# The end of the expert layers: gathers, a combine and key products put in another order

## The chip, the core and the metric

One core of a Trainium2 chip runs the whole program. The metric is the time of one execution on the device in microseconds; less is better. The chip's engines each run their own list of instructions in order and wait for one another through semaphores: TensorE (PE) does matrix products, VectorE (DVE) and ScalarE (ACT) do elementwise work, GpSimd (POOL) small work and the gathers of rows, and the queue of SyncE (SP) starts the transfers from memory.

## The reference

The input x is 625 rows of 512 numbers, with 10,000 edges. Four layers follow, each added to x:

```python
x = x + L0_gnn(layernorm(x), edges)      # two hyperbolic graph convolutions
x = x + L0_ffn(layernorm(x))             # eight experts, two for each row
x = x + L1_gnn(layernorm(x), edges)      # two plain graph convolutions
x = x + L1_ffn(layernorm(x))             # attention over 100 slots and two dense layers
```

The change lies at the end of the second layer and the start of the third. The expert layer is

```python
probs = softmax(xf @ gate_w.T + gate_b); topw, topi = top_k(probs, 2)
sel_w, sel_idx = top_k(wm.T, cap)              # each expert takes its 93 best rows
h = gelu(xg @ w1[e] + b1[e]); out = (h @ w2[e] + b2[e]) * sel_w
of = zeros(T, D).at[sel_idx].add(out)          # rows scattered back
```

with hidden size 2048. A graph convolution of the third layer gathers the normed rows over the edges with degree weights (here a product with a 625 x 628 matrix of edge counts) and multiplies by a 512 x 512 weight. The fourth layer needs, among much else, Wk times a 1024 x 100 matrix, the "keys"; they don't depend on x and are computed early.

## The kernel before, in words

Rows of x are five tiles of 125 (X[:, t, :]). Products in float32 are made of float32r halves: a high half is a copy (ACT), the low half the difference (DVE or POOL), and three products high*high, low*high, high*low are summed in one PSUM bank.

**Experts (`pe_moe`, `a_moe`, `v_moe`, `sp_moe`, `g_moe`).** For expert e there are eight 1 MB weight chunks, four of the first layer (`up(e, c)`, products 8e to 8e+3) and four of the second (`down(e, c)`). `sp_moe` loads chunk m + 8 into the slot of chunk m when `w_used` of m is there; behind the 64th come the two chunks of Wk (`N_TK`), the two weights of the third layer (`N_GNN1`) and four chunks of Wkv. The first six chunks of each expert are split into HW (ACT, high) and LW (DVE, low) by `weights(i)`; the last two are used as they are (down(e, 2) and down(e, 3)). PE's order for an expert is up 0, up 1, gelu 0 (four transposes of HS; ACT's Gelu reads them), up 2, gelu 1, up 3, gelu 2, down 0, gelu 3, down 1, dispatch of the next expert, down 2, gathered_T of the next, down 3. In `scale(e)` DVE adds the bias (OT), ACT multiplies by the gate weight (OS or OW), and for experts six and seven DVE makes the low half (OSL).

**Back to rows.** Experts 0 to 5 (`NB = 6`) write their scaled rows into a DRAM tensor `y_rows`, and since each row has at most two experts, POOL gathers them with two lists of indices: YL (five gathers of 125 rows, the lower expert) and YH (the higher one). DVE adds them to X in `back_low` and `back_high`. Experts 6 and 7 go back through a product with the transposed selection matrix PT, `combine(e)`: two matmuls for each row tile t into bank 3 + t, and DVE adds the bank to X. In before POOL starts YL when the outputs of expert five are written and the ranks of expert seven are known, YH when the gather product of expert seven is done. YL lies where the rank work's tiles were, YH where XFH was. Each engine's list for the last expert is:

- PE: up 0, combine(6), up 1, gelu 0, up 2, gelu 1, up 3, gelu 2, down 0, gelu 3, down 1, down 2, down 3; then keys 0 and 1, combine(7), keys 2 and 3, then `pe_first_aggregate`.
- DVE: combine(6)'s adds, `back_low`, the weights and gelu halves, `degrees`, `back_high`, `v_counts`, scale(7).
- ACT: weights, HS, Gelu, then `a_counts`, scale(7).

**Third layer's start.** CT holds the edge counts; `a_counts` makes GCH and `v_counts` GCL over the expert weights' places HW0 to HW3, and so waits for `w_used`. `v_gnn1` adds combine(7) to X with row sums (`total`), ACT makes squares, POOL the power, DVE the normed rows GU, ACT the high half GTH, DVE the low half GTL. The keys' high and low half A2H and A2L read PSUM bank 0, which is also bank 0 of the aggregate; so the aggregate's work on bank 0 waits for `key_v`. `pe_first_aggregate` goes by row tiles j over the eight banks with GCH, then GCL, and then GTL.

A wait on a semaphore counter is written `q.wait_ge(*count.of(key))`; `landed(n)` is the arrival of load n. PSUM banks are handed on by the dictionary `free`.

Of the kernel before, what the change touches and what calls it, by code (L numbers as in the profile page):

```python
# [130 lines left out]
def program(nc, I, out):  # L131
    T5, P, D, NP = 5, 125, 512, 628
# [8 lines left out]
    with ctx:  # L141
# [9 lines left out]
        place = {}  # L151
# [10 lines left out]
        def after(name):  # L162
            return place[name]
# [77 lines left out]
        def landed(n):  # L241
            return s_raw[slot_of(n)], raw_at[n]
# [825 lines left out]

        def split(m):
            return m % 8 < 6

# [3 lines left out]
        def chunk(i):  # L1077
            return 8 * (i // 6) + i % 6
# [45 lines left out]
        def g_moe(q):  # L1124
            q.wait_ge(*x1_done.of(4))
            g_layernorm(q, ln1, ln_stat, ln_pow, 1)
            q.iota(EO[:, :, :], [[CS, 6], [0, T5]])
            q.fill(LT8[:, :], 1.0)
            q.fill(BIGM[:, :], 1.0)
            q.iota(io94[:, :], [[1, CS]]).then_inc(*mconst.up("one"))  # L1130
            q.wait_ge(*mconst.of("one"))
            q.select(LT8[:, :].rearrange("p (a b) -> p a b", a=8), ALU.is_gt, 0.0, [[1, 8], [-1, 8]], 0)
            q.select(BIGM[:, :], ALU.is_gt, 0.0, [[-1, P]], 1)
            q.fill(io94[:, CAP:CS], -1.0).then_inc(*mconst.up("all"))
            q.wait_ge(*gate_pe.of("lg"))
            q.fill(ZR[:, :], 0.0).then_inc(*mconst.up("zero"))
            q.wait_ge(*code_v.of("low"))
            q.wait_ge(s_wrow, 32)
            q.wait_ge(s_yw[0], 32 * 3)
            q.wait_ge(s_yw[1], 32 * 3)  # L1140
            q.wait_ge(*rank_v.of(NE - 1, "po"))
            for t in range(T5):
                q.gather(YL[:, t, :], yrow, IL[:, t:t + 1]).then_inc(s_rows, 16)
            q.wait_ge(*ga_mm.of(NE - 1))
            for t in range(T5):
                q.gather(YH[:, t, :], yrow, IH[:, t:t + 1]).then_inc(s_back, 16)
# [3 lines left out]
        def a_moe(q):  # L1150
# [95 lines left out]
            for e in range(NE):  # L1246
                n = 6 * e
                up(e, 0)
                weights(n + 4)
                up(e, 1)  # L1250
                gelu(e, 0)
                weights(n + 5)
                up(e, 2)
                gelu(e, 1)
                weights(n + 6)
                up(e, 3)
                gelu(e, 2)
                weights(n + 7)
                gelu(e, 3)
                weights(n + 8)  # L1260
                if e + 1 < NE:
                    dispatch(e + 1)
                    gathered_T(e + 1)
                weights(n + 9)
                if e == NE - 1:
                    a_counts(q)
                scale(e)

        def v_moe(q):
# [209 lines left out]
                q.ts(ln2["rd"], ln2["rd"], 1.0 / D, None, ALU.mult).then_inc(*ln_stat.up(2, "rd"))  # L1479

            def combine(e):
                for t in range(T5):
                    q.wait_ge(*co_mm.of(e, t))
                    q.tt(X[:, t, :], X[:, t, :], PS[0:P, 3 + t, :], ALU.add).then_inc(*x2_done.up(e, t))

# [14 lines left out]
            rank_end(1)  # L1500
            for e in range(NE):
                n = 6 * e
                if e == NE - 1:
                    combine(NE - 2)
                    back_low()
                weights(n + 4)
                gelu(e, 0)
                weights(n + 5)
                if e == NB - 1:
                    places()  # L1510
                if e + 2 < NE:
                    rank_tiles(e + 2, (0, 1))
                gelu(e, 1)
                weights(n + 6)
                if e + 2 < NE:
                    rank_tiles(e + 2, (2, 3))
                weights(n + 7)
                if e + 2 < NE:
                    rank_tiles(e + 2, (4,))
                    rank_end(e + 2)  # L1520
                weights(n + 8)
                if e + 1 < NE:
                    dispatch(e + 1)
                    gathered_T(e + 1)
                weights(n + 9)
                if e == NE - 1:
                    degrees()
                    back_high()
                    v_counts(q)
                scale(e)  # L1530

        def pe_moe(q):
# [123 lines left out]
            def combine(e):  # L1656
                k = e % 2
                q.wait_ge(*os_hi.of(e))
                q.wait_ge(*pt_done.of(e))
                q.wait_ge(*os_lo.of(e))  # L1660
                for t in range(T5):
                    b = 3 + t
                    q.wait_ge(*free[b])
                    q.mm(PS[0:P, b, :], PT[:, k, P * t:P * t + P], OS[:, k, :], True, False)
                    q.mm(PS[0:P, b, :], PT[:, k, P * t:P * t + P], OSL[:, k, :], False, True).then_inc(*co_mm.up(e, t))
                    free[b] = x2_done.of(e, t)
# [7 lines left out]
            gathered_T(0)  # L1674
            for e in range(NE):
                up(e, 0)
                if e == NE - 1:
                    combine(NE - 2)
                up(e, 1)
                gelu(e, 0)  # L1680
                up(e, 2)
                gelu(e, 1)
                up(e, 3)
                gelu(e, 2)
                down(e, 0)
                gelu(e, 3)
                down(e, 1)
                if e + 1 < NE:
                    dispatch(e + 1)
                down(e, 2)  # L1690
                if e + 1 < NE:
                    gathered_T(e + 1)
                down(e, 3)
            pe_keys(q, (0, 1))
            combine(NE - 1)
            pe_keys(q, (2, 3))

# [6 lines left out]
        cols[0] = 0  # L1706
        GCH = at("gCH", [P, T5, NP], f32r, SCR)
        GCL = at("gCL", [P, T5, NP], f32r, after("gCH"))
        GUH = at("gUH", [128, 4, NP], f32r, after("gCL"))
        GUL = at("gUL", [128, 4, NP], f32r, after("gUH"))  # L1710
        GU = at("gU", [P, T5, D], f32, after("gUL"))
# [41 lines left out]
                g_power(q, ln2["rs"][:, t:t + 1], ln2["rs"][:, t:t + 1], hm[0:P, 0:1], ln_pow, 2, t)  # L1753

        def a_counts(q):
            q.wait_ge(*w_used.of(chunk(6 * NE - 1)))
            for m in range(T5):
                q.act(GCH[:, m, :], CT[:, m, :], ACT.Copy).then_inc(*gch_done.up(m))

        def v_counts(q):  # L1760
            q.wait_ge(*w_used.of(chunk(6 * NE - 1)))
            for m in range(T5):
                q.wait_ge(*gch_done.of(m))
                q.tt(GCL[:, m, :], CT[:, m, :], GCH[:, m, :].bitcast(f32), ALU.subtract).then_inc(*gcl_done.up(m))

        def a_gnn1(q):
# [7 lines left out]

            for t in range(3):
                squares(t)
            q.wait_ge(*key_mm.of("a2"))
            q.act(A2H[:, :, :], PS[:, 0, 0:4 * L].rearrange("p (a b) -> p a b", a=4), ACT.Copy).then_inc(*key_a.up("a2"))
            high(0)
            squares(3)  # L1780
            high(1)
            squares(4)
            for t in range(2, T5):
                high(t)
            for k in range(2):
# [17 lines left out]
        def v_gnn1(q):  # L1803
# [28 lines left out]
            total(3)  # L1832
            spread(2)
            normed(1)
            q.wait_ge(*key_a.of("a2"))
            q.tt(A2L[:, :, :], PS[:, 0, 0:4 * L].rearrange("p (a b) -> p a b", a=4), A2H[:, :, :].bitcast(f32), ALU.subtract).then_inc(*key_v.up())
            total(4)
            spread(3)
            normed(2)
            first_low(0)  # L1840
            spread(4)
            normed(3)
            first_low(1)
            normed(4)
            for t in range(2, T5):
                first_low(t)
            for k in range(2):
# [59 lines left out]
        def pe_first_aggregate(q):  # L1907
            def share(b, j, l, r, start, stop):
                f, h = b // 2, b % 2
                return q.mm(PS[:, b, 0:HALF], l[:, j, 128 * f:128 * f + 128], r[:, j, HALF * h:HALF * h + HALF], start, stop)  # L1910

            q.wait_ge(*gcl_done.of(4))
            for j in range(T5):
                q.wait_ge(*th_done.of("g", 0, j))
                for group in (((1, 2, 3, 4, 5, 6), (0, 7)) if j == 0 else (range(8),)):
                    for b in group:
                        if j == 0 and b >= 3:
                            q.wait_ge(*x2_done.of(NE - 1, b - 3))
                        if j == 0 and b == 0:
                            q.wait_ge(*key_v.of())  # L1920
                        share(b, j, GTH, GCH, j == 0, False)
                    for b in group:
                        share(b, j, GTH, GCL, False, False)
            for b in range(8):
                for j in range(T5):
                    q.wait_ge(*tl_done.of("g", 0, j))
                    i = share(b, j, GTL, GCH, False, j == 4)
                if b % 2:
                    i.then_inc(*gu_mm.up(0, b // 2))
# [1022 lines left out]
```

## Time and profile before

| | us |
|---|---|
| median of 3 runs | 2144.78 |
| lowest, highest | 2138.63, 2148.16 |
| the profiled execution | 2148.19 |
| its span, first to last instruction | 2146.4 |
| TensorE busy | 2089.4 (97%) |
| VectorE busy | 1491.4 (69%) |
| ScalarE busy | 1124.4 (52%) |
| GpSimd busy | 872.2 (41%) |

The expert layer takes the stretch from about 180 to 440 us of the span; the last expert from 407 to 440. All times in rows below are microseconds from the span's start, and durations of one instruction or of a merged row of several ("x5"). In square brackets stands how long the engine was idle before, and what released it.

### The profile page before, as it was taken

To read this page: it belongs to the slowest core of one execution; us is meant where nothing else is said; L and a number is where in the kernel's file an instruction comes from. 1 tells how busy PE (TensorE), PEld (TensorE's weight loads), DVE (VectorE), ACT (ScalarE), POOL (GpSimd) and SP (SyncE) were. 2 spreads that over 40 slices of the span, in tenths; PEclk is the share of its full clock that TensorE was granted. 3 is DMA by queue.
4 is the path that set the end of the run, shared out by engine and by line. 5 is a ranking of instruction groups with operands and counts; after the bars stand their busy time and mean duration, and the time that the engine had idled before them with its cause. 6 is when DMAs were issued, how large, how long until landed. Compare 5 with 4: busy or idle time off the path is not lost.

```text
span 2146.4 us, 35992 instructions
## 1 busy us (share of the span) xinstructions
PE 2089.4 (97%) x13282; PEld 1953.0 (91%) x13282; DVE 1491.4 (69%) x3179; ACT 1124.4 (52%) x3010; POOL 872.2 (41%) x704
## 2 busy tenths in 40 slices
PE   8887999998999999999999999999999999999998
PEld 7776666687799999999999999999999999999997
DVE  8656988754366677677666777767667677776676
ACT  4543676534454555555545555555455555554464
POOL 0000000201264555555544555555545555555461
PEclk9887999999999999999999999999999999999999
DMA  6000999940121111132111111222111112221110
GB/s 216 1 29 11 318 324 328 296 166 1 67 87 64 63 63 64 64 103 86 64 64 64 64 64 63 91 96 66 63 63 64 64 63 78 100 75 63 60 45 25
DMA packets 89162, 201.16 MB, mean 94 GB/s; under 512 B 8196, under 2 KB 12580, under 8 KB 88985
## 3 DMA queue, kind: packets, MB, share of 16 engines
q1 hardware_dynamic: 86746, 196.28, 26.9%
q0 software_dynamic: 2240, 2.57, 0.5%
q8 instruction: 106, 1.74, 0.4%
q14 instruction: 70, 0.57, 0.1%
HBM read 196.31 MB, written 2.51 MB: 93 GB/s over the span
## 4 chain that ended last, share of the span: by engine, by line
PE 93%; DVE 3%; DMA 1%; ACT 1%; issue 1%; POOL 0%; SPq 0%; DVEq 0%; POOLq 0%
PE PS L54 84%; PE PS L53 6%; PE PS L57 4%; DMA RAW<-in_L_ffn_w 1%; DMA X<-in_x 0%; DVE OHs L68 0%; DVE OHd L69 0%; DVE JU L66 0%; POOL SM L60 0%; ACT EE L88 0%; DVE ACC L60 0%; DVE SM L60 0%; DVE M L75 0%; DVE SM L75 0%; DVE SM L107 0%
## 5 line engine op out<-in xcount | busy, mean ns | idle before, releaser
L54 PE MATMUL PS<-ZH,WS 128*128 128x314 f32 x4096 | 946.5, 311 | 0.0
L54 PEld LDWEIGHTS PS<-ZH,WS 128*128 128x128 f32 x4096 | 692.3, 189 | 0.0
L54 PE MATMUL PS<-ZL,WS 128*128 128x314 f32 x2048 | 626.1, 306 | 0.0
L60 DVE TENSOR_TENSOR ACC<-ACC,PS 128x314 f32<-128x314 f32 x1008 | 475.9, 477 | 196.9 <-PE PS L54 187.0
L54 PEld LDWEIGHTS PS<-ZL,WS 128*128 128x128 f32 x2048 | 387.6, 189 | 0.0
L60 POOL TENSOR_TENSOR WS<-RAW,WS 128x512 fp32r<-128x512 f32 x256 | 326.5, 1297 | 116.7 <-ACT WS L88 116.7
L60 POOL TENSOR_TENSOR ZS<-ZS,ZQ 128x628 f32<-128x628 f32 x128 | 198.4, 1550 | 230.7 <-ACT ZQ L88 230.4
L60 POOL TENSOR_TENSOR ML<-MF,MH 128x400 fp32r<-128x400 f32 x124 | 130.8, 1055 | 363.7 <-ACT MH L88 363.7
L88 ACT ACTIVATE ZH<-PS,g1T 128x628 fp32r<-128x628 f32 x128 | 100.5, 785 | 313.5 <-PE PS L54 313.5
L88 ACT ACTIVATE EE<-EE,SM 125x100 f32<-125x100 f32 x640 | 233.1, 376 | 0.1
L88 ACT ACTIVATE MF<-PS 128x400 f32<-128x400 f32 x128 | 64.7, 506 | 315.7 <-PE PS L53 315.7
L75 DVE SCALAR_TENSOR_TENSOR ZL<-PS,g1T,ZH 128x628 fp32r<-128x628 f32 x128 | 111.6, 872 | 119.5 <-ACT ZQ L88 119.5
L60 POOL TENSOR_TENSOR WQ<-RAW,WQ 128x512 fp32r<-128x512 f32 x128 | 168.2, 1314 | 41.0 <-ACT WQ L88 41.0
L60 DVE TENSOR_TENSOR EE<-PS,CB 125x400 f32<-125x400 f32 x160 | 91.9, 575 | 132.1 <-PE PS L54 131.5
L60 DVE TENSOR_TENSOR EE<-EE,SM 125x500 f32<-125x500 f32 x128 | 154.3, 1205 | 4.4
L88 ACT ACTIVATE WS<-RAW 128x512 fp32r<-128x512 f32 x256 | 147.6, 633 | 0.0
L88 ACT ACTIVATE ATH<-PS 100x500 fp32r<-100x500 f32 (+1 forms) x256 | 96.6, 430 | 93.4 <-PE PS L57 93.4
L54 PE MATMUL PS<-MH,XH 128*125 128x400 f32 x640 | 144.1, 347 | 0.1
L54 PE MATMUL PS<-MH,XL 128*125 128x400 f32 x640 | 143.4, 346 | 0.0
L54 PE MATMUL PS<-ML,XH 128*125 128x400 f32 x640 | 142.4, 344 | 0.0
L60 DVE TENSOR_TENSOR LW<-RAW,HW 128x1024 fp32r<-128x1024 f32 x96 | 112.8, 1219 | 29.2 <-ACT HW L88 29.1
L53 PEld LDWEIGHTS PS<-KCL,WQ 128*128 128x128 f32 x1024 | 130.4, 192 | 2.2 <-issue 2.0
(357 smaller groups left out, 3580.5 us busy)
## 6 DMA issues: line engine op xcount, KB each, us to landing
RAW<-in_L_ffn_wz_w SPq DMA_DIRECT2D x66, 1024.0 KB, 6.0
RAW<-in_L_ffn_w SPq DMA_DIRECT2D x64, 1024.0 KB, 6.4
RAW<-in_L_ffn_Wq_w SPq DMA_DIRECT2D x32, 1024.0 KB, 8.5
CB<-c_rows SPq DMA_DIRECT2D x32, 195.3 KB
RAW<-in_L_gnn_W SPq DMA_DIRECT2D x4, 1024.0 KB, 11.4
RAW<-in_L_ffn_Wkv_w SPq DMA_DIRECT2D x4, 1024.0 KB, 9.4
RAW<-in_L_ffn_Wk_T SPq DMA_DIRECT2D x2, 1024.0 KB, 14.9
WB<-w_rows SPq DMA_DIRECT2D x6, 273.4 KB
```

The source lines that it names most:

```text
L53: return self.q.matmul(o, l, r, start=start, stop=stop, skip_group_check=True)
L54: return self.q.matmul(o, l, r, start=start, stop=stop)
L57: return Nothing() if self.q is None else self.q.transpose(o, i, idn)
L60: return Nothing() if self.q is None else self.q.tensor_tensor(out=o, in0=a, in1=b, op=op)
L75: return self.q.scalar_tensor_tensor(out=o, in0=a, scalar=s, in1=b, op0=op0, op1=op1)
L88: return self.q.activation(o, i, f, **kw)
```

## The change

1. POOL waits, before the first YL gather, also for the landing of the last expert's last weight chunk.
2. combine(6) moves on PE from behind up(7, 0) to behind up(7, 3), with the row tiles in the order 3, 0, 1, 2, 4; DVE's adds of it and the YL adds move behind all weight and gelu work of expert seven.
3. `a_counts` moves ahead of the third Gelu of expert seven and waits for up(7, 3)'s weights; `v_counts` moves ahead of `back_high`, and waits by tile for the weights in whose place it writes.
4. One key group runs before combine(7) and three behind it, instead of two and two; A2H and A2L come later on ACT and DVE; the aggregate's bank 0 is done after the second tile's other banks.

```diff
@@ program
+        turn = (3, 0, 1, 2, 4)
@@ g_moe
             q.wait_ge(*rank_v.of(NE - 1, "po"))
+            q.wait_ge(*landed(N_MOE + 8 * NE - 1))
             for t in range(T5):
                 q.gather(YL[:, t, :], yrow, IL[:, t:t + 1]).then_inc(s_rows, 16)
@@ a_moe, loop over experts
                 up(e, 3)
+                if e == NE - 1:
+                    a_counts(q)
                 gelu(e, 2)
...
                 weights(n + 9)
-                if e == NE - 1:
-                    a_counts(q)
                 scale(e)
@@ v_moe
             def combine(e):
-                for t in range(T5):
+                for t in turn:
...
-                if e == NE - 1:
-                    combine(NE - 2)
-                    back_low()
                 weights(n + 4)
...
                 if e == NE - 1:
+                    combine(NE - 2)
                     degrees()
+                    back_low()
+                    v_counts(q)
                     back_high()
-                    v_counts(q)
                 scale(e)
@@ pe_moe
-                for t in range(T5):
+                for t in (turn if e == NE - 2 else range(T5)):
...
                 up(e, 0)
-                if e == NE - 1:
-                    combine(NE - 2)
                 up(e, 1)
                 gelu(e, 0)
                 up(e, 2)
                 gelu(e, 1)
                 up(e, 3)
+                if e == NE - 1:
+                    combine(NE - 2)
                 gelu(e, 2)
...
-            pe_keys(q, (0, 1))
+            pe_keys(q, (0,))
             combine(NE - 1)
-            pe_keys(q, (2, 3))
+            pe_keys(q, (1, 2, 3))
@@ a_counts, v_counts
-            q.wait_ge(*w_used.of(chunk(6 * NE - 1)))
+            q.wait_ge(*w_used.of(chunk(6 * NE - 3)))
...
-            q.wait_ge(*w_used.of(chunk(6 * NE - 1)))
             for m in range(T5):
+                q.wait_ge(*w_used.of(chunk(6 * NE - (2 if m < 4 else 1))))
                 q.wait_ge(*gch_done.of(m))
@@ a_gnn1
             for t in range(3):
                 squares(t)
-            q.wait_ge(*key_mm.of("a2"))
-            q.act(A2H...)
             high(0)
             squares(3)
             high(1)
             squares(4)
+            q.wait_ge(*key_mm.of("a2"))
+            q.act(A2H...)
@@ v_gnn1
             normed(1)
-            q.wait_ge(*key_a.of("a2"))
-            q.tt(A2L...)
             total(4)
             spread(3)
             normed(2)
-            first_low(0)
             spread(4)
             normed(3)
+            q.wait_ge(*key_a.of("a2"))
+            q.tt(A2L...)
+            normed(4)
+            first_low(0)
             first_low(1)
-            normed(4)
@@ pe_first_aggregate, inside the loop over j
-                for group in (((1, 2, 3, 4, 5, 6), (0, 7)) if j == 0 else (range(8),)):
-                    ...
+                for b in range(1, 8):
+                    if j == 0 and b >= 3:
+                        q.wait_ge(*x2_done.of(NE - 1, b - 3))
+                    share(b, j, GTH, GCH, j == 0, False)
+                for b in range(1, 8):
+                    share(b, j, GTH, GCL, False, False)
+                if j == 1:
+                    q.wait_ge(*key_v.of())
+                for i in ((), (0, 1), (2,), (3,), (4,))[j]:
+                    share(0, i, GTH, GCH, i == 0, False)
+                    share(0, i, GTH, GCL, False, False)
```

## Rows read from the trace of the kernel before

**Rows 1.** The page, part 1: busy time of TensorE and its weight loads.
```profile
PE 2089.4 (97%) x13282; PEld 1953.0 (91%) x13282; DVE 1491.4 (69%) x3179; ACT 1124.4 (52%) x3010; POOL 872.2 (41%) x704
```

**Rows 2.** Chain of work that ended last, 340 to 480: start us, us, what.
```profile
391.25 16.51 DMA RAW<-in_L_ffn_w
```

**Rows 3.** Timeline of TensorE: start us, us, engine, line, operation, out<-in, count [idle before].
```profile
410.25 0.40 PE L54 MATMUL PS<-LW,XGH 128*94 128x512 f32 x1
413.52 0.46 PE L54 MATMUL PS<-OS,PT 94*125 94x512 f32 x1 [2.87 <-DVE OSL L75]
...
415.66 0.63 PE L54 MATMUL PS<-OS,PT 94*125 94x512 f32 x1
...
439.49 3.71 PE L54 MATMUL PS<-aw,RAW 128*128 128x100 f32 x32
442.98 0.47 PE L54 MATMUL PS<-OS,PT 94*125 94x512 f32 x1
...
450.27 1.11 PE L54 MATMUL PS<-gCH,gTH 125*128 125x314 f32 x6 [1.20 <-ACT gTH L88]
```

**Rows 4.** Timeline of GpSimd: first gather of each list, and the last one.
```profile
386.51 1.43 POOL L125 DMA_INDIRECT YL<-y_rows,IL  x1 [203.01 <-issue]
...
400.98 1.21 POOL L125 DMA_INDIRECT YH<-y_rows,IH  x1 [6.31 <-PE PS L54]
...
407.26 1.21 POOL L125 DMA_INDIRECT YH<-y_rows,IH  x1 [0.30 <-issue]
```

**Rows 5.** Transfers, 386 to 422: queue, packets, MB, share; issues, KB, us to landing.
```profile
q1 hardware_dynamic: 3910, 7.72, 75.1%
q0 software_dynamic: 2240, 2.57, 30.7%
...
RAW<-in_L_ffn_w SPq DMA_DIRECT2D x6, 1024.0 KB, 19.0
```

**Rows 6.** Transfers, 422 to 444: packets, MB, mean rate.
```profile
DMA packets 4250, 8.46 MB, mean 384 GB/s; under 512 B 128, under 2 KB 128, under 8 KB 4249
```

**Rows 7.** Single transfers, issued in 382-384, 384-387, 407-409: KB, us to landing.
```profile
RAW<-in_L_ffn_w SPq DMA_DIRECT2D x1, 1024.0 KB, 5.3
RAW<-in_L_ffn_w SPq DMA_DIRECT2D x1, 1024.0 KB, 6.1
YH<-y_rows,IH POOLq DMA_INDIRECT x1, 14.4
```

**Rows 8.** The gathers' queue in 404 to 410 and in 410 to 416.
```profile
q0 software_dynamic: 401, 0.43, 29.5%
q0 software_dynamic: 517, 0.60, 41.0%
```

**Rows 9.** Timeline of SyncE's queue: last expert chunk, and the Wkv chunks.
```profile
407.91 1.40 SPq L128 DMA_DIRECT2D RAW<-in_L_ffn_w  x1
429.73 10.32 SPq L128 DMA_DIRECT2D RAW<-in_L_ffn_Wkv_w  x4
```

**Rows 10.** Timeline of VectorE.
```profile
427.11 3.10 DVE L60 TENSOR_TENSOR X<-X,YH 125x512 f32<-125x512 f32 x5
433.65 3.70 DVE L60 TENSOR_TENSOR gCL<-CT,gCH 125x628 fp32r<-125x628 f32 x5 [3.44 <-ACT gCH L88]
439.69 0.69 DVE L60 TENSOR_TENSOR OT<-PS,B 94x512 f32<-94x512 f32 x1 [2.33 <-PE PS L54]
441.17 0.75 DVE L75 SCALAR_TENSOR_TENSOR OSL<-OT,SM,OS 94x512 fp32r<-94x512 f32 x1 [0.79 <-ACT OS L88]
```

**Rows 11.** Timeline of ScalarE.
```profile
400.53 2.00 ACT L88 ACTIVATE HW<-RAW 128x1024 fp32r<-128x1024 f32 x2 [4.59 <-DMA RAW<-in_L_ffn_w]
...
432.82 3.20 ACT L88 ACTIVATE gCH<-CT 125x628 fp32r<-125x628 f32 x5 [1.73 <-PE PS L54]
...
447.11 0.19 ACT L88 ACTIVATION_READ_ACCUMULATOR gU<-X,SM 125x1 f32 x1
```

**Rows 12.** Windows: busy us of PE, PEld, DVE, ACT, POOL; granted clock, DMA share, GB/s.
```profile
190.00:195.00 5.00, 4.09 (x20) 2.99 (x19) 4.20 (x16) 2.70 (x5) 0.00 (x0) 0.67 0.00 2
```

## What the change does to the time, predicted from the trace of before

> **What bounds the kernel now.** I read the page first: TensorE is busy 97% of the span [rows 1], so time is won or lost only where TensorE stands still or runs slowly, or where its work changes. The change keeps the count of matrix products; it moves them. The chain of work that ended last, around the experts' end, is TensorE's own work, except for one stretch that goes back to a weight chunk's transfer issued at 391.25 us, 16.5 us long [rows 2]. The timeline of TensorE shows what that costs. The last matmul of the first quarter of expert seven's first layer (called up(7,0) in the code) starts at 410.25; the next, expert six's combine, starts at 413.52 after an idle time of 2.87 us that VectorE's OSL ends. Behind it a matmul takes 0.63 us (415.66) where the same one takes 0.39 at 410.25; in the timeline they start 0.43 us apart instead of 0.23, from 414.97 to 418.6. Further on: 439.49 first two key groups, 442.98 combine of expert seven, and 450.27 the next layer's first aggregate, after 1.20 us of waiting for ACT's gTH [rows 3].
>
> Then the transfers. POOL issues the five YL gathers from 386.51 and the five YH gathers from 400.98 to 407.26 [rows 4]. Between 386 and 422 the two queues together move 7.72 and 2.57 MB, 10.29 MB in 36 us or 286 GB/s [rows 5]; right after it, with no gather, 384 GB/s [rows 6]. One weight chunk of 1 MB lands in 5.3 to 6.1 us just before the gathers; the last YH gather takes 14.4 us to land [rows 7]. ACT sits idle 4.59 us for a chunk that the gathers held up [rows 11]. This is the delay behind the OSL wait: chunk, HW, LW, OT, OS, OSL.
>
> **The change, part by part.**
>
> (a) **Combine(6) goes behind up(7,3).** Its ten matmuls stay. The 2.87 us idle time goes, since up(7,1) needs only its own chunk and XGL. So does the slow clock that followed: nine matmuls at 0.43 instead of 0.23 us, 1.7 us. The end of down(7,3), where the keys start at 439.49 [rows 3], comes 4.6 us earlier: 434.9. In its new place the combine waits for nothing: OS, OSL and PT are long there, bank 6 comes first in the new order because the next transpose wants it, and VectorE's adds (3.2 us for five) run beside it. Nothing is late next: the weight chunks, no longer beside gathers, land in about 6 us.
>
> (b) **Counts' halves.** ACT copies GCH (3.20 us [rows 11]) now between HS and the third gelu of expert seven; down(7,2) comes about 6 us after that gelu's transpose, so this is covered. VectorE's GCL (3.70 us [rows 10]) moves between the YL adds and the YH adds; it fills waiting time. Cost nothing.
>
> (c) **Gathers wait for the last weights.** What stands behind this wait on POOL is all ten gathers; who waits for them is VectorE: the YL adds, then GCL, then the YH adds, then OT of expert seven, in this order in its queue. OT in turn releases OS, OSL and combine(7) on TensorE. In the kernel before the YH adds stood at 427.11 and OT at 439.69 [rows 10], with some 9 us to spare. Now:
> - The last chunk is issued at 407.91 in the trace of before, behind down(6,3) [rows 9]; TensorE has no stall before that, so the issue stays at about 407.6 (the row's 0.3 us later is SP's own). It lands 5.3 to 6.1 us later [rows 7]: 413.2.
> - The ten gathers, from the first issue to the last landing, took 407.26 + 14.4 - 386.51 = 35.2 us [rows 4, 7]. Was that because YH was only issued at 400.98? No: the gathers' queue moves 0.43 MB in 404 to 410 and 0.60 in 410 to 416 [rows 8], 70 to 100 KB per us, and the ten gathers' 2.57 MB at 80 KB per us fill the time from 390 to 421, so it was their rate beside the weights' queue that set it. Is the weights' queue as full in the new place? The loads that run then are the rest of the two key chunks, two GNN chunks and four KV chunks (0.7 + 2.1 + 4.2 = 7.0 MB), issued as expert seven's quarters finish; in before the last four go out from 429.73 to 440 [rows 9], now some 5 us earlier. The weights' queue moved at most 7.72 MB in 36 us, 0.21 MB per us, beside gathers [rows 5]; from 417 to 448 that is 6.6 MB. So it never runs dry, and I take the same 35.2 us: the last YH row lands at 413.2 + 35.2 = 448.4.
> - YH adds 3.04 us (five, back to back [rows 10]), then OT to OSL's end, 441.92 - 439.69 = 2.23, and 0.14 to TensorE's start: combine(7) at 453.8. TensorE has run out of work at 434.9 + 1.75 (one key group; two take 442.98 - 439.49 = 3.5 [rows 3]) = 436.6. It stands 17 us.
> - Bounds: if the gathers had the transfer engines for themselves, POOL's issuing alone takes 15.5 us (two times five, 1.5 each [rows 4]) and the last lands some 2 to 3 us later: 18 us, the lower bound. The upper bound is 35.2 plus the 4 us by which the first gather's bytes came after its issue, and a last chunk 1 us later: 40. I take 35.2, for it is the same ten gathers beside the same kind of load.
>
> (d) **Keys one before, three behind the combine.** This takes away the 1.20 us wait for gTH: behind combine(7)'s start come 2.38 us of combine and 5.25 us of keys, 7.6 us, and the first aggregate can begin, since ACT now makes GTH before A2H (in before the third row tile's squares end at 447.30 [rows 11], 4.3 us after combine(7) started; with 0.6 us for the copy GTH is there after 4.9). Before it was 450.27 - 442.98 = 7.3 us. Bank 0's shares move behind the second round, where A2L is there; their count stays 80 for the first two kinds. Cost nothing.
>
> (e) **Clock.** After a long idle time TensorE works at half clock: in 190 to 195 us, where it resumed after 6.8 us, the granted clock was 0.67, that is about 3.3 us at the lower level [rows 12]. Work of half that time is lost: 1.7 us.
>
> **Sum.** First aggregate at 453.8 + 7.6 + 1.7 = 463.1 instead of 450.27: +12.8 us. Everything behind is TensorE's work in a 97% busy program [rows 1], with GNN chunks in place by 434 (some 30 us before they are copied), so the shift stays. The profiled execution was 2148.2 us (span 2146.4), so its like would be 2161.0; the median of the runs shown is 3.4 us lower, 2144.8, and the forecast is 2144.8 + 12.8 = 2157.6 us.
>
> One rule of the Trainium skill speaks for less. The page "DMA: Bandwidth & Descriptors", section "Anatomy of one DMA", gives 2.0 us plus bytes over 436 GB/s for a POOL-issued DMA. By it, an estimate, the 2.57 MB would need 5.9 us of moving and hide inside POOL's issuing, and the sum would be that of rival 1; the 14.4 us of the last YH gather [rows 7] speaks against it where weights run beside. The same page, section "Queues, rings and completion order", has each engine take its queues in turn by packets, which agrees with the rows and would hold in the new place too.
>
> **Rivals.**
> 1. *Gathers hidden* (not slower). If the gathers' queue gets much more of the engines because the weights' queue is less deep than in 388 to 410, where chunks took 19 us to land, the rows come within 18.7 us of the wait's end (by 431.9). Then OT follows down(7,3) at 435.0, combine(7) starts at 437.3, the aggregate at 444.9: -5.3 us, 2139.5. For it: expert seven's chunks are issued 3.1 us apart, and 1 MB takes 2.7 us at 384 GB/s [rows 6], so a queue that was first empty stays shallow. Against: it is not empty from the moment gathers take a third of the engines' time [rows 5].
> 2. *Partly hidden.* The break-even is at a last landing of 437.3, 24 us after the first issue (437.3 + 5.4 + 7.6 = 450.3). Gathers of 24 to 30 us give 0 to +8 us (clock loss with it): 2145 to 2153.
> 3. *More than forecast.* The last chunk late, gathers behind a fuller queue, 40 us: +17, 2162.
> 4. *The change doesn't do what it says:* the wait is passed at once because the last chunk has landed. No: the gathers started at 386.51, the chunk is issued 21 us later [rows 4, 9]. I give it nothing.
>
> **How the numbers follow.** Forecast case 0.68, rival 2 0.17, rival 1 0.08, rival 3 0.07. The forecast's own range is 2153 to 2162: the gathers' 33 to 38 us and 2 us for a median (the three runs of before lie 9.5 us apart). The range for 8 in 10 reaches down into rival 2 and up into rival 3: 2146 to 2164. A measurement of this kernel can tell about 0.5%, 10.7 us, from no change. Slower by more than that: seven in ten of the forecast case (0.48) and rival 3 (0.07), 0.55. Faster by more needs rival 1 with luck in the medians: 0.03. Same: the rest, 0.42.
>
> **What would show it.** In the profile after: no idle time on TensorE between up(7,0) and down(7,3), whose end is near 434.9, and full clock there; chunks of expert seven landing in about 6 us; the first YL gather at 413; combine(7) released by OSL, behind YH adds that start at 448, and a TensorE idle time of 17 us before it; matmuls at half clock for 3 us after. Wrong would be gathers that land in under 24 us in all, or an idle time ahead of combine(7) under 5 us; or a new wait at combine(6), the third gelu or the first aggregate that is not named here.

## The result, and the profile after

The changed kernel took 2162.0 us (median of 4 runs, 2153.4 to 2171.6) against 2143.8 us of the kernel before (4 runs, 2138.6 to 2148.2). The ratio is 1.0081, with a 95% interval from 1.0053 to 1.0109: slower by 0.8%, some 18 us, with 11 to 23 us in the interval. The forecast was 2157.6 us: 12.8 us more than 2144.8, the median of three runs that it started from.

The profiled execution of the changed kernel was its fastest, 2153.4 us with a span of 2151.6. So its span is only 5.2 us longer than the one of before, and the two spans don't show what the change did. Runs of one kernel lie up to 22 us apart; what differs between them stands in the last section. I therefore read all traces below by one stretch that holds everything the change touches: from U, the end of up(7,0), to the start of the first aggregate (the first matmul that reads gCH and gTH). U is the start of up(7,0)'s last matmul plus the 0.23 us by which these follow one another, or, which is the same, the start of the next matmul where none is late. In the kernel before it is 410.25 + 0.23 = 410.48, and the aggregate starts at 450.27 [rows 3]: 39.8 us.

TensorE after (start us, us, engine, line, operation, out<-in, count, idle time before and its releaser):

```profile
404.64 0.40 PE L54 MATMUL PS<-HW,XGH 128*94 128x512 f32 x1
...
413.37 0.39 PE L54 MATMUL PS<-LW,XGH 128*94 128x512 f32 x1
413.61 0.39 PE L54 MATMUL PS<-OS,PT 94*125 94x512 f32 x1
...
422.13 7.03 PE L54 MATMUL PS<-RAW,GT 128*94 128x512 f32 x16
429.00 1.92 PE L54 MATMUL PS<-aw,RAW 128*128 128x100 f32 x16
448.60 0.76 PE L54 MATMUL PS<-OS,PT 94*125 94x512 f32 x1 [17.68 <-DVE OSL L75]
449.16 0.63 PE L54 MATMUL PS<-OSL,PT 94*125 94x512 f32 x1
...
453.00 5.90 PE L54 MATMUL PS<-aw,RAW 128*128 128x100 f32 x48
458.67 1.26 PE L54 MATMUL PS<-gCH,gTH 125*128 125x314 f32 x7
```

Up(7,1) starts at 404.64, which is U here. Combine(6) (413.61) follows up(7,3) with no idle time, the matmuls from up(7,1) to combine(6) take 0.39 to 0.45 us each, and down(7,3) is done at 429.0, U + 24.4. The 2.87 us of idle time and the slow matmuls of [rows 3] are gone. Then TensorE does one key group and stands idle 17.68 us. The stretch is 458.67 - 404.64 = 54.0 us: 14.2 us longer. Ahead of U this execution was 5.8 us shorter than the one of before, and behind the aggregate 3.2 us shorter (1692.9 against 1696.1); that is how 14.2 us became 5.2 in the span.

What it waits for is in the chain of work that ended last (start us, us, what):

```profile
402.06 5.33 DMA RAW<-in_L_ffn_w
...
408.43 1.63 POOL YL L125
...
423.29 19.90 DMA YH<-y_rows,IH
...
446.95 0.73 ACT OS L88
447.68 0.03 issue
447.70 0.76 DVE OSL L75
448.46 0.14 issue
448.60 26.31 PE PS L54 x168
```

The last weight chunk, then POOL's ten gathers one behind the other, then 19.90 us for the last YH gather to land, then VectorE, ACT, VectorE, TensorE. Between the chunk's landing (407.39) and the first gather (408.43) lies 1.04 us in which POOL waited for nothing that the profile shows. VectorE's timeline has the queue behind the gathers:

```profile
429.04 3.10 DVE L60 TENSOR_TENSOR X<-X,YL 125x512 f32<-125x512 f32 x5 [11.18 <-DMA YL<-y_rows,IL]
432.06 3.70 DVE L60 TENSOR_TENSOR gCL<-CT,gCH 125x628 fp32r<-125x628 f32 x5
443.22 3.10 DVE L60 TENSOR_TENSOR X<-X,YH 125x512 f32<-125x512 f32 x5 [7.46 <-DMA YH<-y_rows,IH]
446.23 0.68 DVE L60 TENSOR_TENSOR OT<-PS,B 94x512 f32<-94x512 f32 x1
```

In the kernel before the YH adds stood at 427.11 and OT waited for TensorE [rows 10]; now OT waits for the YH adds. The transfers in the window 408 to 444 (queue: packets, MB, share; then issues, KB, median us to landing):

```profile
q1 hardware_dynamic: 3683, 7.32, 73.5%
q0 software_dynamic: 2240, 2.57, 31.0%
...
RAW<-in_L_ffn_Wkv_w SPq DMA_DIRECT2D x4, 1024.0 KB, 18.7
```

It is nearly the picture of [rows 5] again, 31% of the engines' time for the gathers, with the Wkv chunks in the place of expert seven's. The windows show TensorE's clock (busy us of PE, PEld, DVE, ACT, POOL; granted clock, DMA share, GB/s):

```profile
436.00:440.00 4.00, 0.00 (x0) 0.00 (x0) 0.00 (x0) 0.00 (x0) 0.00 (x0) 0.50 1.08 246
...
448.00:452.00 4.00, 3.40 (x8) 2.74 (x9) 2.53 (x9) 1.22 (x3) 0.16 (x1) 0.50 0.00 0
452.00:456.00 4.00, 4.00 (x27) 3.70 (x27) 3.61 (x15) 3.83 (x10) 2.65 (x4) 0.77 0.01 3
456.00:460.00 4.00, 4.00 (x35) 4.00 (x35) 1.16 (x4) 1.11 (x4) 0.90 (x2) 1.00 0.57 193
```

From the start of combine(7) to the first aggregate it took 458.67 - 448.60 = 10.1 us.

Expert seven's chunks, no longer beside gathers, landed in 5.2 to 6.8 us here (six of them, issued from 382.29 on), as the prediction said.

### The profile page after: what moved, and what is told of

Read it like the earlier page. It is cut to its first block, busy times and chain, and to the rows that moved or that the text cites. A ratio compares the mean times of both kernels' runs of the same rounds, so it can differ in the third digit from the quotient of the medians.

```text
span 2151.6 us, 35993 instructions
## 1 busy us (share of the span) xinstructions
PE 2082.9 (97%) x13282; PEld 1946.7 (90%) x13282; DVE 1491.7 (69%) x3179; ACT 1123.6 (52%) x3010; POOL 871.3 (40%) x704
## 3 DMA queue, kind: packets, MB, share of 16 engines
q1 hardware_dynamic: 86746, 196.28, 26.8%
## 4 chain that ended last, share of the span: by engine, by line
PE 92%; DVE 3%; DMA 2%; ACT 1%; POOL 1%; issue 1%; SPq 0%; DVEq 0%; POOLq 0%
PE PS L54 83%; PE PS L53 5%; PE PS L57 4%; DMA YH<-y_rows,IH 1%; DMA X<-in_x 0%; POOL YL L125 0%; DVE OHs L68 0%; POOL SM L60 0%; DVE SM L107 0%; DMA RAW<-in_L_ffn_w 0%; ACT EE L88 0%; DVE JU L66 0%; POOL YH L125 0%; DVE OHd L69 0%; DVE ACC L60 0%
## 5 line engine op out<-in xcount | busy, mean ns | idle before, releaser
L53 PE MATMUL PS<-KCL,WQ 128*128 128x200 f32 (+1 forms) x1024 | 128.5, 268 | 0.8 <-DVE KCL L60 0.4
```

The lines of the kernel that those rows point to most:

```text
L53: return self.q.matmul(o, l, r, start=start, stop=stop, skip_group_check=True)
```

## The experiments

The stretch in each, all from one profiled execution, and the ratio to the kernel before where runs were timed:

| kernel | U | first aggregate | stretch | ratio (95%) |
|---|---|---|---|---|
| before | 410.48 | 450.27 | 39.8 | |
| changed | 404.64 | 458.67 | 54.0 | 1.0081 (1.0053 to 1.0109) |
| e1_no_wait | 405.11 | 442.00 | 36.9 | 0.9989 (0.9967 to 1.0010) |
| e2_hold_loads | 410.57 | 452.18 | 41.6 | 1.0004 (0.9984 to 1.0024) |
| e3_kept_busy | 405.55 | 459.65 | 54.1 | |
| e4_keys_only | 405.66 | 444.68 | 39.0 | 0.9992 (0.9969 to 1.0014) |
| e5_wait_59 | 410.81 | 445.40 | 34.6 | 0.9988 (0.9968 to 1.0009) |
| e6_wait_alone | 405.08 | 461.38 | 56.3 | 1.0082 (1.0061 to 1.0103) |
| e7_high_list_late | 409.93 | 455.23 | 45.3 | |
| e8_kept_busy_longer | 402.36 | 455.66 | 53.3 | |

**Without the wait (e1_no_wait).**

```diff
             q.wait_ge(*rank_v.of(NE - 1, "po"))
-            q.wait_ge(*landed(N_MOE + 8 * NE - 1))
             for t in range(T5):
                 q.gather(YL[:, t, :], yrow, IL[:, t:t + 1]).then_inc(s_rows, 16)
```

> The changed kernel without the wait of the gathers for the last weight chunk; all else of the change stays. Theory (the late gathers are the whole loss): the YL gathers start where they did before, the YH rows land before the last expert is done, and the 17.7 us of idle time ahead of combine(7) go. From the end of up(7,0) to the first aggregate the kernel before took 39.8 us and the changed one 54.0; here 34 to 38, because the weight chunks come late again and one of them may stop TensorE for about 2 us ahead of combine(6). Against before: 2 to 5 us faster. Rival (the loss is in the moved combine, counts or keys): the stretch stays above 42 us.

The stretch is 36.9 us, 17.1 less than in the changed kernel and 2.9 less than before. So the wait is the whole loss and the rest of the change, which moves the combine, the counts and the keys, gains; the rival falls. Timed, it can't be told from the kernel before (ratio 0.9989, interval 0.9967 to 1.0010). The cost of early gathers is still there, at another place. ScalarE and TensorE in this run:

```profile
413.56 2.01 ACT L88 ACTIVATE HW<-RAW 128x1024 fp32r<-128x1024 f32 x2 [1.43 <-DMA RAW<-in_L_ffn_w]
...
417.00 0.50 PE L54 MATMUL PS<-OS,PT 94*125 94x512 f32 x1 [0.58 <-ACT GT L88]
418.67 0.52 PE L57 MATMUL PS<-ident,HS 94*128 94x94 f32 x4 [0.93 <-DVE X L60]
```

ACT splits expert seven's sixth chunk late (U + 8.5, against U + 4.3 in the changed kernel), its gelu behind it is late, and the last tile of combine(6) and the transposes of the third gelu wait 0.58 and 0.93 us.

**The loads behind the experts held back (e2_hold_loads).**

```diff
             for m in range(64):
                 q.wait_ge(*w_used.of(m))
+                if m == 58:
+                    q.wait_ge(s_back, 16 * T5)
                 load(q, N_MOE + 8 + m)
```

> The changed kernel, with one more wait: SyncE's queue holds the six loads behind the two key chunks (two GNN weights, four Wkv chunks) until all ten gathers have landed. Theory (the gathers are slow because they share the transfer engines with weights): from the first issue to the last landing 18 to 22 us instead of 34.8, idle time ahead of combine(7) under 3 us, stretch from the end of up(7,0) to the first aggregate 35 to 38 us instead of 54.0, 3 to 5 us faster than before. Rival (gathers of rows are slow by themselves): still some 35 us and the same 54.

Here is the first gather, VectorE's YH adds that wait for the last, and in the window 421 to 434 what the gathers' queue moved with no weights beside it:

```profile
414.38 1.61 POOL L125 DMA_INDIRECT YL<-y_rows,IL  x1 [230.84 <-issue]
```

```profile
435.12 3.10 DVE L60 TENSOR_TENSOR X<-X,YH 125x512 f32<-125x512 f32 x5 [1.13 <-DMA YH<-y_rows,IH]
```

```profile
q0 software_dynamic: 1720, 2.05, 50.3%
```

The ten gathers took 435.1 - 414.4 = 20.7 us instead of 34.8, and 2.05 MB went in 13 us, 158 KB per us, about twice the 80 beside weights. So what makes them slow is the traffic of the weights' queue, as expected; they then go about as fast as POOL issues them (1.5 us each), and each lands 4.0 to 5.7 us after its issue. But TensorE still stood 3.64 us ahead of combine(7), 0.6 more than I allowed, and the stretch was 41.6 us, not 35 to 38, and 1.8 longer than before:

```profile
440.50 0.76 PE L54 MATMUL PS<-OS,PT 94*125 94x512 f32 x1 [3.64 <-DVE OSL L75]
...
444.90 7.51 PE L54 MATMUL PS<-aw,RAW 128*128 128x100 f32 x48
```

The three key groups took 7.5 us where they take 5.5 at full clock; from combine(7) to the aggregate it was 11.7 us. The granted clock was 0.50 all through 440 to 448. Less the 7.6 us that this piece takes at full clock, that is 4.1 us lost to the clock behind 3.64 us of idle time, more than behind the 17.68 us of the changed kernel.

**TensorE kept busy (e3_kept_busy, e8_kept_busy_longer).**

```diff
             pe_keys(q, (0,))
+            pe_busy(q, 1, XGH[:, :, :].rearrange("p a b -> p (a b)"), 70)    # 84 in the second
             combine(NE - 1)
```

> The changed kernel with 70 matmuls on TensorE between the first key group and combine(7), whose results nobody reads. They fill the idle time (70 x 0.23 = 16.1 us) and keep the clock up. Theory: from the start of combine(7) to the first aggregate 7.6 us instead of 10.1, so 2.4 us of the loss are the clock's; the start of combine(7) doesn't move. Rival (the slow stretch behind the idle time is something else, such as waits for VectorE's adds): still 10 us.

With 70 it came out at 9.3 us, not 7.6: the fill ended too early, 2.2 us of idle time were left, and the clock, still full at the restart, fell 1.1 us after it. Combine(7) also started at U + 44.8, 0.9 us later than in the changed kernel, where I had expected no move. The clock's part needs a run without idle time, so a second one has a longer fill. Combine(7) in this run:

```profile
450.37 0.47 PE L54 MATMUL PS<-OS,PT 94*125 94x512 f32 x1 [2.20 <-DVE OSL L75]
450.68 0.39 PE L54 MATMUL PS<-OSL,PT 94*125 94x512 f32 x1
...
452.19 0.63 PE L54 MATMUL PS<-OS,PT 94*125 94x512 f32 x1
```

> As the run with 70 matmuls between the first key group and combine(7), now 84, whose results nobody reads. With 70 TensorE still stood idle 2.2 us ahead of combine(7) and then ran at 0.43 us per matmul for 3 us. Theory (idle time of 2 us or more ahead of the combine brings the clock down): with no idle time left, matmuls of combine(7) start 0.23 us apart, and its start to the first aggregate is 7.6 to 7.9 us instead of 9.3 (70) and 10.1 (none). Rival: the combine runs slow all the same, 9 us or more.

With 84 there is no idle time and no slow matmul:

```profile
448.09 0.39 PE L54 MATMUL PS<-OS,PT 94*125 94x512 f32 x1
...
450.39 5.50 PE L54 MATMUL PS<-aw,RAW 128*128 128x100 f32 x48
455.66 1.27 PE L54 MATMUL PS<-gCH,gTH 125*128 125x314 f32 x7
```

7.6 us from combine(7) to the aggregate, as expected. So 2.5 of the 10.1 us are the clock's. The fill was longer than needed: OSL was ready 2.4 us before combine(7), so the stretch itself, 53.3 us, gains little.

**The keys' part alone (e4_keys_only).** The kernel before, with `pe_keys` 1 and 3 and the new order in `a_gnn1`, `v_gnn1` and `pe_first_aggregate`:

```diff
-            pe_keys(q, (0, 1))
+            pe_keys(q, (0,))
             combine(NE - 1)
-            pe_keys(q, (2, 3))
+            pe_keys(q, (1, 2, 3))
```

> The kernel before with only the keys' part of the change: one key group ahead of combine(7) and three behind, A2H and A2L later, bank 0 of the aggregate behind the second tile. Theory: the 1.20 us wait for gTH goes, but combine(7) now waits for OSL (0.8 us of idle time); from the start of combine(7) to the first aggregate 7.6 us instead of 7.3, combine(7) starts 0.9 us earlier; stretch from the end of up(7,0) 39.2 us instead of 39.8: 0.6 us faster, which only the trace can show.

The stretch was 39.0 us, 0.8 less than before. The wait for gTH is gone, and TensorE waits 0.65 us for OSL ahead of combine(7) (436.99). This is as expected (39.2), and not to be seen in timed runs (0.9992, 0.9969 to 1.0014).

**The wait alone (e6_wait_alone).** The kernel before with the one line that e1_no_wait takes out.

> The kernel before with the gathers' wait alone; the moved combine, counts and keys are left out. The YL adds then stand in VectorE's list ahead of expert seven's weight and gelu work. Theory: VectorE waits for YL until U + 22, so down(7,0) can't start before U + 28, and the YH adds, GCL and OT end near U + 46; first aggregate at U + 53 to 57 instead of 39.8, with most of the idle time ahead of down(7,0) instead of combine(7). 13 to 17 us slower than before. Rival (only the YH list counts, and the moved combine is what costs): near U + 40 to 45.

```profile
429.05 3.10 DVE L60 TENSOR_TENSOR X<-X,YL 125x512 f32<-125x512 f32 x5 [20.06 <-DMA YL<-y_rows,IL]
```

```profile
435.37 0.71 PE L54 MATMUL PS<-HW,GEH 128*94 128x512 f32 x1 [18.36 <-DVE LW L60]
```

The stretch is 56.3 us, 16.5 more than before; timed, 1.0082 (1.0061 to 1.0103). VectorE stands 20 us at the YL adds, with expert seven's weight halves behind them, and TensorE 18.36 us ahead of down(7,0). So the wait costs about the same in the old order of work (16.5 us) as in the new one (17.1), and all the rest of the change, put around it, takes back only 2.3 us.

**An earlier chunk to wait for (e5_wait_59).**

```diff
-            q.wait_ge(*landed(N_MOE + 8 * NE - 1))
+            q.wait_ge(*landed(N_MOE + 8 * NE - 5))
```

> The changed kernel with the gathers waiting for the landing of expert seven's fourth weight chunk instead of its eighth (U is the end of up(7,0)). Theory (what decides is the last landing, 35 us after the first issue, against the 32 us from now on at which it is first needed): first gather near U - 13, last landing near U + 22, YH adds done at U + 25 when down(7,3) is; no idle time over 1 us in the last expert, combine(7) at U + 27.5, first aggregate at U + 35.0, against 39.8 before, 54.0 changed, 36.9 without the wait. 5 us faster than before in the trace; the median may hide half of it. Rival (early gathers always cost what they cost in the kernel before, by late chunks): idle time ahead of combine(6) or of a gelu stays at 1.5 us or more, stretch 36.5 to 38.

```profile
398.71 2.18 POOL L125 DMA_INDIRECT YL<-y_rows,IL  x1 [214.90 <-issue]
```

```profile
431.56 3.10 DVE L60 TENSOR_TENSOR X<-X,YH 125x512 f32<-125x512 f32 x5 [0.92 <-DMA YH<-y_rows,IH]
435.38 0.69 DVE L60 TENSOR_TENSOR OT<-PS,B 94x512 f32<-94x512 f32 x1 [0.71 <-PE PS L54]
```

```profile
437.75 0.47 PE L54 MATMUL PS<-OS,PT 94*125 94x512 f32 x1 [0.65 <-DVE OSL L75]
```

First gather at U - 12.1, YH landed at U + 20.8 (32.9 us), combine(7) at U + 26.9 behind 0.65 us of idle time, the only one over 0.5 us in the stretch. OT waits for TensorE again, not for the YH adds. The stretch is 34.6 us long: 5.2 us less than before, 2.3 less than without the wait, 19.4 less than changed. The same wait, four chunks earlier, is a small gain instead of a loss. Timed, the ratio is 0.9988 (0.9968 to 1.0009): 5 us are 0.24%, which 12 runs can't tell from nothing. That it beats the kernel before is shown by this stretch of one execution alone, not by the times.

**Only the second list late (e7_high_list_late).** The gathers' wait stands ahead of the YH gathers instead of the YL gathers.

> The changed kernel with YL gathered as early as before and only the five YH gathers waiting for the last weight chunk. Theory (each list takes 15 to 18 us beside weights, lists queue behind one another): YH issued at U + 4, landed at U + 20 to 23, in time; no idle time ahead of combine(7) over 2 us; first aggregate at U + 34.5 to 37. Rival (a gather that starts after the last chunk is late whatever stands before it): landed at U + 30 or later, first aggregate at U + 47 or later.

```profile
417.99 1.26 POOL L125 DMA_INDIRECT YH<-y_rows,IH  x1 [23.89 <-DMA RAW<-in_L_ffn_w]
```

```profile
438.41 3.10 DVE L60 TENSOR_TENSOR X<-X,YH 125x512 f32<-125x512 f32 x5 [8.57 <-DMA YH<-y_rows,IH]
```

My expectation was wrong: 45.3 us, between the two values expected. Five gathers took 20.4 us, somewhat over the 15 to 18 said; above all they were issued at U + 8.1, not U + 4. I had taken the last chunk's landing from a queue without gathers, but the early YL gathers delay the weights, and so the very chunk that the YH gathers now waited for: it landed 9.8 us after its issue, against 5.3 in the changed kernel.

## Why the prediction was right

**The gathers (step c), the term that decides.** First issue predicted at 413.2, U + 2.7; in fact it was 408.43, U + 3.8. The chunk itself landed where it was expected (407.39, U + 2.75); the 1.04 us from there to the first gather had been put at nothing. From first issue to last landing predicted 35.2 us, measured 443.19 - 408.43 = 34.8. This rested on the claim that the weights' queue would be as full in the new place, and that its fullness sets the rate: e2_hold_loads shows the second half (20.7 us with the loads held), the transfer rows above the first. The lower bound of 18 us counted 2 to 3 us from the last issue to its landing; no run shows so little, and with the loads held the last gather took 5.7. YH adds to combine(7) were put at 5.4 us, measured 448.60 - 443.22 = 5.4. The idle time was predicted at 17.2 us and measured at 17.68.

**The moved combine (step a).** Down(7,3) ends at U + 24.4 as predicted (434.9 - 410.48). One thing was said too simply: that a combine in the new place waits for nothing holds because the gathers no longer hold up the chunks. With early gathers (e1_no_wait) the combine and the transposes behind it wait 1.5 us for the gelu and the adds.

**Counts (b) and keys (d).** The counts cost nothing: GCL ran in VectorE's wait for YH, GCH beside TensorE's combine. Keys: combine(7) to aggregate without the clock's part 7.6 us, predicted 7.6 (e8_kept_busy_longer); alone they gain 0.8 us (e4_keys_only), which was not worked out as a sum in the prediction.

**The clock (e)** was sized too low: 1.7 us predicted, 2.5 measured by the difference of the changed kernel and e8_kept_busy_longer. The price taken from one restart [rows 12] is not a constant: it was 2.5 us behind 17.68 us of idle time, 4.1 behind 3.64 (e2_hold_loads), 3.8 behind 7.57 (e7_high_list_late: combine(7) at 443.79, aggregate at 455.23, less 7.6), 1.7 behind 2.20 (e3_kept_busy). What it depends on is how long TensorE works at the lower level. Read in windows of 1 us, that was 5.2 us in the changed kernel, 8.6 in e2_hold_loads, 8.1 in e7_high_list_late and 3.4 in e3_kept_busy; half of each is 2.6, 4.3, 4.0 and 1.7 us, which are the losses within 0.2. The trace of before already held a dearer restart than the one that the prediction read, at 200.46 behind 2.98 us of idle time, with 6.4 us of work at the lower level:

```profile
200.00:205.00 5.00, 4.54 (x14) 3.36 (x15) 3.40 (x13) 0.00 (x0) 0.00 (x0) 0.51 0.27 63
```

**Sum.** Predicted stretch 463.1 - 410.5 = 52.6 us, measured 54.0; +12.8 against +14.2. The 1.4 us are, rounded, the later first issue (1.1) and the clock (0.8), less 0.4 of the gathers. The timed +18.2 us has 14.2 in its interval of 11 to 23; where the other 4 us come from, if they are real, is not settled. The median, 2162.0, is the very number that the prediction gave to rival 3 (gathers of 40 us), and close to the upper end of its range, 2164. The trace has the gathers at 34.8 us, so the mechanism is the forecast's and not rival 3's; with four runs 18 us apart it took some luck that the median stayed inside the range. E6_wait_alone, whose stretch is 16.5 longer, was timed at +17.2 (2159.4 against 2142.2).

**The rivals.** Rivals 1 and 2, gathers hidden or partly hidden, fell on the full weights' queue. The threshold of rival 1, a last landing by U + 21.4 (431.9 - 410.5) costs nothing, fits e5_wait_59, which at U + 20.8 paid nothing. The break-even of rival 2, a last landing at U + 26.8 (437.3 - 410.5), did not hold: in e2_hold_loads the last row landed at U + 24.5 and the stretch was still 1.8 us longer than before, because that sum had no term for the clock and the clock took 4.1 us. The rule from the Trainium skill, "DMA: Bandwidth & Descriptors", section "Anatomy of one DMA" (2.0 us plus bytes over 436 GB/s), would give, as an estimate, 2.6 us for one gather of 256 KB. The traces have 7.8 to 19.9 us in the changed kernel, beside weights, and 4.0 to 5.7 us in e2_hold_loads with the loads held. The measurement decides: the formula is no price for these gathers, least of all beside a full queue. The section "Queues, rings and completion order" of the same page has each transfer engine take its queues in turn, by packets. The trace agrees while both queues are full; in the window 424 to 436 of the changed kernel they moved nearly as many packets:

```profile
q1 hardware_dynamic: 941, 1.87, 66.9%
q0 software_dynamic: 937, 1.10, 39.5%
```

A packet of the gathers held 1.2 KB (1.10 MB in 937), one of the loads 2.0 KB. So the gathers got half of the packets but 37% of the bytes, 92 KB per us against 158 with the loads held.

## What to carry to other kernels

A transfer that disturbs others shouldn't simply be put behind the last of them: ask when its result is first needed, subtract what it takes beside the traffic that will then run, and start it there. Here 33 to 35 us of gathers, needed at U + 21, had to start by about U - 12 to U - 14. Three kernels differ in this start alone: at U - 12 the stretch was 34.6 us (e5_wait_59), at U - 24 it was 2.3 longer (e1_no_wait), at U + 4 19.4 longer (the changed kernel). And where a late result stands in the middle of an engine's ordered list, price all that is queued behind it, down to the engine that sets the end.

## What was not expected of the hardware

**The clock can stay low in a busy stretch, and the scatter of the runs goes with it.** The profiled execution of e5_wait_59 had the shortest stretch of all and still a span of 2150.3 us. Its windows, then the same work in the kernel before:

```profile
536.00:546.00 10.00, 9.41 (x57) 8.12 (x56) 1.04 (x4) 1.92 (x4) 0.00 (x0) 0.78 0.01 2
546.00:556.00 10.00, 10.00 (x44) 9.29 (x44) 2.31 (x6) 2.45 (x6) 0.00 (x0) 0.50 0.16 43
556.00:566.00 10.00, 10.00 (x36) 9.20 (x36) 2.67 (x5) 2.95 (x6) 2.55 (x2) 0.52 0.00 0
```

```profile
550.00:560.00 10.00, 10.00 (x75) 9.22 (x75) 4.32 (x8) 6.03 (x13) 1.28 (x1) 1.00 0.14 44
```

TensorE was busy 10 of 10 us in both by the profile's count, at 1.2 GHz in the one for some 20 us and at 2.4 GHz in the other. Behind the first aggregate this execution took 2150.3 - 445.4 = 1704.9 us, the one of before 2146.4 - 450.3 = 1696.1: 8.8 us more for the same code. The clock accounts for it: in 500 to 600 us it was 0.83 against 0.90 of before and in 600 to 700 0.98 against 1.00, together about 9 us of work at full clock; from 700 to 2100 us it was 1.00 in both. Ahead of U the ten profiled executions differ by 8.5 us (402.36 to 410.81), though TensorE's work there is the same. Between the kernel before and e4_keys_only, whose gathers too are alike there, it is 4.8 us, and 4 of them are the clock's (0.84 and 0.95 against 0.86 and 0.97 in 100 to 200 and 200 to 300). The timed runs go the same way: the 12 of e5_wait_59 reach from 2132.9 us at a mean clock of 0.986 to 2152.2 at 0.978. Why the clock differs from run to run is open. So one span can't show a change of 5 or even 14 us in this kernel, and the short stretch can.

**A shorter idle time can cost more than a long one**: 3.64 us of it were followed by 4.1 us of loss, 17.68 by 2.5. TensorE restarted at half clock in both; the full clock was back 8.6 us after the restart in the one and 5.2 us in the other. Why was not tested.
